# The fill of the window phase: first values into the score banks, second sequence turned behind them, group statistics in later periods

## The reference, cut to what matters

```
x = layernorm(h)                       # no scale: the group statistics of this document
for l in range(2):
    q, k, v = split(shift_token(x) @ wqkv[l])
    q, k = rotary_xpos(l2norm(q) * qs, l2norm(k) * ks)
    x = x + softmax(mask(8 * q @ k.T)) @ v @ wo[l]
    a, g = split((layernorm(shift_token(x)) * lg + lb) @ w1[l] + b1[l])
    x = x + (a * gelu(g)) @ w2[l] + b2[l]
```

## Time and profile before

| what | us |
|---|---|
| median of 3 runs | 1328.47 |
| lowest and highest | 1324.59, 1329.86 |
| profiled execution | 1324.94 |
| its span, first to last instruction | 1323.2 |
| mean granted TensorE clock | 0.981 |

### The profile page before, as it was taken

How to read it: one execution, slowest core, us unless ns; L and a number is a source line. 1 busy time by engine, 2 the same in 40 slices (tenths; PEclk the granted TensorE clock), 3 DMA queues, 4 the chain that set the end, 5 groups by cost and what they waited for, 6 DMA issues and landing times.

```text
span 1323.2 us, 26280 instructions
## 1 busy us (share of the span) xinstructions
PE 1237.8 (94%) x9027; PEld 1055.8 (80%) x9027; DVE 975.9 (74%) x2609; ACT 866.0 (65%) x1987; POOL 629.6 (48%) x694
## 2 busy tenths in 40 slices
PE   5899999999999998899977889999999999999996
PEld 4799889889988987777755667888888887888786
DVE  5767666766667675998887897778778788777633
ACT  2455766675566654889943567677777787777753
POOL 7423431341235233555234567556656567666442
PEclk9899999999999999999987999999999999999999
DMA  7300010010000001110020002000100000000000
GB/s 167 110 1 14 1 63 0 14 63 0 0 8 1 1 1 57 17 55 10 17 68 1 1 5 84 11 5 5 48 4 3 20 5 13 21 21 21 21 17 25
DMA packets 35489, 33.19 MB, mean 25 GB/s; under 512 B 12474, under 2 KB 32050, under 8 KB 35378
## 3 DMA queue, kind: packets, MB, share of 16 engines
q1 hardware_dynamic: 34482, 29.65, 7.5%
q0 software_dynamic: 768, 2.10, 0.9%
q10 hardware_dynamic: 128, 0.04, 0.0%
HBM read 25.75 MB, written 4.19 MB: 23 GB/s over the span
## 4 chain that ended last, share of the span: by engine, by line
PE 44%; DVE 7%; issue 4%; POOL 3%; ACT 3%; DVEq 0%; ACTq 0%; POOLq 0%
PE w_ps_p L1866 3%; PE w_ring L1926 3%; PE w_ring L1927 3%; PE w_ring L1928 3%; PE w_ring L1836 2%; PE w_ring L1838 2%; PE w_ring L1837 2%; PE w_ps_a L1884 2%; PE w_ps_d L1859 2%; PE w_ps_d L1856 2%; PE w_ring L1938 2%; PE a_ps L903 2%; PE w_ring L1843 2%; PE w_ring L1939 1%; PE w_ring L1940 1%
## 5 line engine op out<-in xcount | busy, mean ns | idle before, releaser
L377 ACT ACTIVATE t_gf<-t_ps_f,t_fb_cur 128x512 f32<-128x512 f32 x128 | 87.9, 687 | 169.9 <-PE t_ps_f L283 166.7
L296 PE MATMUL t_ps_o<-t_w_hi,t_g_hi 128*128 128x256 f32 x512 | 146.7, 287 | 3.3 <-DVE t_g_lo L527 3.2
L527 DVE TENSOR_TENSOR t_g_lo<-t_gf,t_g_hi 128x512 fp32r<-128x512 f32 x128 | 93.8, 735 | 70.6 <-ACT t_g_hi L379 69.4
L298 PE MATMUL t_ps_o<-t_w_hi,t_g_lo 128*128 128x256 f32 x512 | 145.3, 284 | 0.0
L297 PE MATMUL t_ps_o<-t_w_lo,t_g_hi 128*128 128x256 f32 x512 | 145.3, 284 | 0.0
L680 POOL TENSOR_TENSOR t_rs<-t_ve,t_neghalf 128x4 f32<-128x4 f32 x32 | 35.0, 1094 | 170.8 <-DVE t_ve L488 169.3
L2431 DVE COPY w_pt<-w_ps_p 128x384 f32<-128x384 f32 x128 | 70.5, 551 | 62.0 <-PE w_ps_p L1866 60.6
L1926 PE MATMUL w_ring<-w_nh,w_w_hi 128*128 128x256 f32 x352 | 104.2, 296 | 6.9 <-DVE w_nl L2475 5.2
L2652 POOL TENSOR_TENSOR w_m<-w_m 128x512 f32<-128x512 f32 x64 | 85.5, 1336 | 40.2 <-DVE w_m L2388 40.1
L296 PEld LDWEIGHTS t_ps_o<-t_w_hi,t_g_hi 128*128 128x128 f32 x512 | 98.3, 192 | 7.8 <-issue 4.5
L281 PE MATMUL t_ps_f<-t_nh,t_w_hi 128*128 128x512 f32 x256 | 102.7, 401 | 1.4 <-DVE t_nl L503 1.0
(11 more groups left out here) (310 smaller groups left out, 4324.8 us busy)
## 6 DMA issues: line engine op xcount, KB each, us to landing
t_raw<-in_L_tok_w SPq DMA_DIRECT2D x8, 1024.0 KB
out<-X SPq DMA_DIRECT2D x14, 256.0 KB, 2.1
raw<-in_L_ffn_wqkv SPq DMA_DIRECT2D x2, 1536.0 KB, 6.6
raw<-in_L_ffn_w SPq DMA_DIRECT2D x4, 640.0 KB, 4.9
w_raw_o<-out SPq DMA_DIRECT2D x8, 256.0 KB, 2.8
w_xs<-X SPq DMA_DIRECT2D x14, 127.0 KB
w_raw<-in_L_ffn_w SPq DMA_DIRECT2D x2, 640.0 KB
t_raw_d<-in_L_tok_D SPq DMA_DIRECT2D x4, 256.0 KB
```

Of the source, the lines that this page charges most:

```text
L296: pe.matmul(out, g_hi[:, j % 4, tok], w2_hi[:, j, :], start=(j == 0 and t % 2 == 0), stop=False, skip_group_check=True)
L298: mm = pe.matmul(out, g_lo[:, j % 4, tok], w2_hi[:, j, :], start=False, stop=(j == FC - 1 and t % 2 == 1), skip_group_check=True)
L527: dve.tensor_tensor(g_lo[:, j % 4, :], gf[:, j % 2, :], g_hi[:, j % 4, :].bitcast(F32), ALU.subtract).then_inc(g_split, 1)
```

## The change

1. In period 1 the values of item 0 go into the two score banks (`first_values`), right behind the last key projection, and no longer wait for the rotation. ACT takes them from there (`keep_first`).
2. The turning of item 1 follows at once; ACT `spread(1, 0)` stands ahead of `root(0, 1)`, DVE `split_in(1, 0)` ahead of `inverse_root(0, 1)`, and PE's first query projection of item 1 moves from the start of period 2 to the end of period 1, ahead of the turning of the first keys of item 0.
3. In period 2 the two value projections of item 1 stand behind `scores(1)` and `scores(2)` instead of behind `scores(3)`.
4. Group statistics: `x0_variance(2)` from period 1 to period 2 (behind the inverse roots), `x0_norm(2)` to period 3; `x0_variance(3)` from period 3 to 5, `x0_norm(3)` to period 6; `x0_root(2)` and `x0_root(3)` on POOL accordingly.
5. `fills` is split: the array of maxima is cleared in period 1, the padding in period 2 (`fill` then counts to 2).
6. `hi_2(0)` moves from period 5 to the end of period 4, `lo_2(0)` from period 5 to period 4, between `scale_p(12)` and `scale_p(13)`.
7. Some waits are added where a bank now has another reader before it.

```diff
@@ tensor
+            def first_values(t):
+                tok = slice(t * P, (t + 1) * P)
+                cols = slice(2 * INNER, 3 * INNER)
+                pe.wait_ge(done["y_added"], NSQ)
+                for c in range(DC):
+                    pe.matmul(ps_d[:, t, :], ah[:, c, tok], qkv_hi[:, c, cols], start=(c == 0), stop=False)
+                    pe.matmul(ps_d[:, t, :], ah[:, c, tok], qkv_lo[:, c, cols], start=False, stop=False)
+                    mm = pe.matmul(ps_d[:, t, :], al[:, c, tok], qkv_hi[:, c, cols], start=False, stop=(c == DC - 1))
+                mm.then_inc(S["v_full"], 1)
...
-                if real(b):
-                    pe.wait_ge(S["split1"], b + 1)
+                if real(b) and h != 2:
                     pe.wait_ge(S["split1"], b + 1)
                     project(b, 0, 0, 0, "q_full")
...
+                    pe.wait_ge(S["k_read"], 2 * c + 2)
...
+                        pe.wait_ge(S["q_read"], 2 * c + 2)
...
+                    pe.wait_ge(S["v_done"], 2 * c + 2)
...
                     scores(NU * c + 1)
+                if h == 2:
+                    pe.wait_ge(S["k_read"], 2 * b + 2)
+                    project(b, 0, 2, 3, "v_full")
...
                     scores(NU * c + 2)
+                if h == 2:
+                    pe.wait_ge(S["q_read"], 2 * b + 2)
+                    project(b, 1, 2, 2, "v_full")
...
-                if real(b):
+                if h == 1:
+                    first_values(0)
+                    first_values(1)
+                elif real(b) and h != 2:
                     ...
                     project(b, 0, 2, 3, "v_full")
...
-                if real(b):
+                if real(b) and h > 2:
                     ...
                     project(b, 1, 2, 2, "v_full")
+                if h == 1:
+                    pe.wait_ge(S["split1"], 2)
+                    project(a, 0, 0, 0, "q_full")
@@ scalar
+            def keep_first(t):
+                act.wait_ge(S["v_full"], t + 1)
+                act.activation(v[:, t, :], ps_d[:, t, :], ACT.Copy).then_inc(S["v_done"], 1)
...
+                if h == 1:
+                    keep_first(0)
+                    keep_first(1)
+                    spread(1, 0)
                 if real(b):
                     root(b, 1)
...
-                if h == 5:
-                    hi_2(0)
...
                     turned(b, 0, 1, 1)
+                if h == 4:
+                    hi_2(0)
@@ vector
                     add_attention(e, 0)
+                if h == 6:
+                    x0_norm(3)
...
                     clamp(b, 1)
+                if h == 1:
+                    fill_maxima()
+                if h == 3:
+                    x0_norm(2)
+                if h == 5:
+                    x0_variance(3)
...
+                if h == 1:
+                    split_in(a, 0)
                 if real(b):
                     inverse_root(b, 1)
                 if real(d):
                     output_lo(NU * d + 3)
+                if h == 2:
+                    x0_variance(2)
                 if real(c):
                     turned_p(H * c + 2)
-                if real(a):
+                if h == 2:
+                    fills()
+                if real(a) and h != 1:
                     split_in(a, 0)
...
-                if h == 1:
-                    x0_variance(2)
-                if h == 1:
-                    x0_norm(2)
-                if h == 3:
-                    x0_variance(3)
-                if h == 3:
-                    x0_norm(3)
@@ gpsimd
-                if h == 1:
-                    x0_root(2)
                 if real(b):
                     scale_k(b, 1)
+                if h == 5:
+                    x0_root(3)
                 if 0 <= f < M - 1:
                     hidden_lo(f, 0)
-                if h == 5:
-                    lo_2(0)
...
                 if real(b):
+                    if h == 2:
+                        x0_root(2)
                     scale_p(NU * b + 0)
+                    if h == 4:
+                        lo_2(0)
                     scale_p(NU * b + 1)
```

More of the change, by code:

```diff
@@ L2124, in hi_2 @@
                 act.wait_ge(S["h_used"], NSQ * FC * l)
-                act.wait_ge(S["fill"], 1)
+                act.wait_ge(S["fill"], 2)
                 act.activation(w2_hi[0:LAST, FC - 1, :], raw_2[0:LAST, FC - 1, :], ACT.Copy)
@@ L2316, in half @@
                     output_hi(NU * d + 3)
-                if real(b):
+                if real(b) and h != 1:
                     keep_values(b, 0, 3)
@@ L2612, in fills @@
             def fills():
-                dve.wait_ge(done["y_full"], NSQ)
                 for w in (w1_hi, w1_lo):
@@ L2618, in fills, with fill_maxima @@
                 for w in (w2_hi, w2_lo):
-                    dve.memset(w[:, FC - 1, :].bitcast(F32), 0.0)
+                    ins = dve.memset(w[:, FC - 1, :].bitcast(F32), 0.0)
+                ins.then_inc(S["fill"], 1)
+            def fill_maxima():
+                dve.wait_ge(done["y_full"], NSQ)
                 dve.memset(mx[:, :, :], 0.0).then_inc(S["fill"], 1)
                 dve.wait_ge(S["fill"], 1)
-            return half, pads, table, fills, x0_variance, x0_norm, split_in, rotate
+            return half, pads, table, x0_variance, x0_norm, split_in, rotate
         def gpsimd(pool):
@@ L2716, in half @@
                     hidden_lo(f, 1)
-                if h == 3:
-                    x0_root(3)
                 if h == 8:
@@ L2865, in _ @@
                 early_half, _, first = a_vector(dve)
-                half, pads, table, fills, x0_variance, x0_norm, split_in, rotate = w_vector(dve)
+                half, pads, table, x0_variance, x0_norm, split_in, rotate = w_vector(dve)
                 first()
@@ L2880, in _ @@
                 rotate(0, 0, 1, 1)
-                half(1)
-                fills()
-                for h in range(2, M3 + 6):
+                for h in range(1, M3 + 6):
                     half(h)
```

## The result

The changed kernel takes 1313.02 us (median of 4 runs, 1308.42 to 1315.75) against 1328.66 for the kernel before (4 runs, 1324.59 to 1329.86): a ratio of 0.989, interval 0.986 to 0.992. It is faster, by 1.1%, and the forecast of 1312 is 1 us off, closer than runs that spread over 7 us can tell. Timed again later it gave 1312.97 (6 runs) against 1325.82, ratio 0.990 (0.988 to 0.993). The profiled execution took 1310.7 with a span of 1308.9, 14.3 less than the profiled execution before, where the sum of the prediction was 14.8.

A forecast was written before the change was run, and what follows sets the result against it. PE was taken as the bound from period 6 on, with the fill's gain moving everything behind it. Terms 7.6 + 4.9 - 1.2 + 3.5 = 14.8 us gave 1310.1 or 1313.7; forecast 1312 us, range 1307 to 1321.

The forecast's parts named there:

- The values and the first projection of item 1: Period 1: PE can project item 1 at 697.1 where it started at 702.14, 5.0 us earlier.
- Rotation of item 1: Period 2: DVE starts to rotate item 1 at 700.5 instead of 707.1, 6.6 us earlier.
- `split_in` of item 2 at about 722: End of period 2: item 2 split at about 722 instead of 730.07; fill gain taken as 7.6 us.
- the low-clock rival: Clock stays low in the new fill, which then brings only 3.0 us; 1314.7 to 1318.3 us, chance 0.17.
- Group 3: Period 3 into 4: its statistics and normalization no longer precede the softmax; gain 4.9 us (3.2 to 4.9).
- `hi_2`: Period 4: ACT's copies ahead of item 4's first squares delay DVE's rotations; loss 1.2 us (0 to 1.9).
- `lo_2`: Period 5: it no longer holds back `scale_p(14)`, removing PE's 2.04 us wait and low clock; gain 3.5 us (2.0 to 3.7).
- `x0_variance(3)` and `x0_norm(3)`: Periods 5 and 6: the moved pieces cost 0, up to 1.2 us and up to 2.1 us respectively.
- `x0_norm(2)`: Period 3: needs 1.38 us and fits where DVE is idle for 2.11 us, ahead of 750.76.
- the skeptical case: Period 3: by the port-lock rule the moved normalization could take 2.1 us or start late; 2.1 still fits into 2.11.
- the one with the wait for `split1`: Period 1: this wait on item 1 replaces the removed one; 7.2 us less gain, 1318 to 1321 us, chance 0.05.
- the one with DVE as the bound: DVE bounds the whole start and moved pieces come back; 8.4 us less gain, or 3.8 left, 1321 to 1324; chance 0.12.

The follow-up runs named there:

- values alone: Kernel before with only item 0's values moved into the score banks, without the earlier turning and with group 2 where it was: 1325.1 us, ratio 0.997.
- the second trace: Changed kernel run once more, unchanged, on the chip of a later comparison: 1312.97 us, ratio 0.990 to the kernel before.
- both halves: Changed kernel with hi_2(0) and lo_2(0) put back in period 5: 1319.53 us, ratio 0.994 to the kernel before.
- best version: Changed kernel with group 2's statistics, root and fills in period 3, normalization in period 4: 1309.03 us, ratio 0.985; again 1310.37 us, ratio 0.987.
- the kernel with the low half back: Changed kernel with only lo_2(0) back in period 5, hi_2(0) staying in period 4: 1315.54 us, ratio 0.991 to the kernel before.

## Why the prediction was right, step by step

- *The values and the first projection of item 1* were to start at 697.1; they did at 696.91, with 1.74 us of wait where 1.9 was worked out. Putting the values back into the ring brings PE's 3.65 us back. Right.
- *Rotation of item 1* at 700.5, measured 700.16; *first softmax* at 706.9, measured 706.19. Right, within 0.7 us. That it needs group 2 gone was shown twice: with the values alone the second interval gives back 2.6 of 4.0 us, and group 2 back in period 1 costs a 3.24 us wait and the clock.
- *`split_in` of item 2 at about 722*, measured 721.69 + 0.40 = 722.09, a gain of 8.0. The working had come to 8.1 and took 7.6 of it without saying why. In part this was luck: `soft` began 0.7 earlier than worked out, and from there to the end of the split it took 15.9 us instead of 15.0. What I did not count is what happens right behind: the hole of 716 to 722 leaves a clock of 0.66 for 5 us and the next wait (1.71 us at 738.01) one of 0.76 for 7 us. Item 3 is split only 6.8 us earlier (748.7 against 755.5), and only 5.6 in the second trace (750.0). The term was too large by 0.8, or by 2.0, and no step of mine had this; the low-clock rival had the mechanism, but in the stretch before.
- *Group 3*, 4.9 taken: the wait at 797.59 stands at 786.54, 11.05 us earlier, which is 4.2 more than at item 3's split (4.6 in the second trace); putting it back cost 4.4 to 4.8. Mechanism right, size 0.1 to 0.7 too large.
- *`hi_2`*, a loss of 1.2 taken: nothing was lost. The wait of PE is 0.95 us at 786.54 against 0.96. The rows for this stand below the list.
- *`lo_2`*, 3.5 taken: the span is 14.3 us shorter and the scores at 799.04 came 11.0 earlier, so 3.3; by the fifth and sixth intervals it is 3.6, and 3.6 in the kernel with that edit alone. Right in this pair of traces; "values alone" shows that about 1.5 of it is a low clock that need not come. It ran at 794.86 to 798.46 in POOL's idle time (795.55, 2.91 us), and PE waited 0.26 us behind it, as at this place before. The step did not say that this gain and the free place of `x0_root(3)` depend on each other; undoing `lo_2` costs 4.8, and both halves 5.7, not 3.5.
- *`x0_variance(3)` and `x0_norm(3)`* at no cost: the fifth and later intervals are those of the kernel that has group 3 elsewhere (31.6 and 35.9 in both). *`x0_norm(2)`* took 2.17 us at 741.79, beside POOL's two scalings from 741.24, as the skeptical case had it (2.1), and no wait of PE of more than 0.22 us follows up to 752.54: right, though no run moved it alone.

  The rule of the Trainium skill, SBUF — State Buffer, section "Who interferes with whom", that DVE and GpSimd lock each other out of a shared port pair, agrees with this row and with the 1.22 us that 16 elements took at 697.45 beside POOL's 1.30 from 697.34.
- *The sum.* 6.8 + 4.2 + 0 + 3.3 = 14.3, against 7.6 + 4.9 - 1.2 + 3.5 = 14.8. Three terms were 0.2 to 0.8 too large, and one loss of 1.2 did not come, so the sum is nearer than its parts. That it is only 0.5 off is luck; the steps are right by their mechanism and to about 1 us each. Of the rivals, the one with the wait for `split1` is out (1.74 us, not 3.67), the one with DVE as the bound is out for the later periods, but true of one place, the hole in period 2, worth 3.5 to 4.6 us.
- *Readings of the rows.* Two were slightly off, without weight in the sum: one of PE's waits in period 2 (0.73 us at 710.45 before) was not for DVE, and the two small steps behind the statistics took 0.38 and 0.47 us at 756.87 before, not 0.55 together.

The delay by `hi_2` was there at first. Item 4's first rotation starts at 778.72, 9.99 us earlier than in the kernel before (788.71), while ScalarE's rounding just ahead of it (773.53 against 784.65) came 11.1 earlier: it is 1.1 late. It was won back a few rows on. The kernel before, VectorE and then GpSimd, in period 4:

```profile
793.89 1.00 DVE L2471 SCALAR_TENSOR_TENSOR w_nmr<-w_mv,w_rs 128x2 f32<-128x2 f32 x1
794.82 0.66 DVE L2396 TENSOR_SCALAR w_sc<-w_ss 128x16 f32<-128x16 f32 x1
795.58 0.69 DVE L2376 TENSOR_REDUCE w_ss<-w_m 128x8 f32<-128x512 f32 x1
```

```profile
792.36 2.51 POOL L2652 TENSOR_TENSOR w_m<-w_m 128x512 f32<-128x512 f32 x2
```

The changed kernel, VectorE, the same three pieces of work:

```profile
783.76 0.59 DVE L2504 SCALAR_TENSOR_TENSOR w_nmr<-w_mv,w_rs 128x2 f32<-128x2 f32 x1
784.27 0.16 DVE L2429 TENSOR_SCALAR w_sc<-w_ss 128x16 f32<-128x16 f32 x1
784.54 0.69 DVE L2409 TENSOR_REDUCE w_ss<-w_m 128x8 f32<-128x512 f32 x1
```

Two tiny operations on DVE took 1.00 and 0.66 us before, and 0.59 and 0.16 after. Before, the first ended at 794.89, as POOL's 2.51 us from 792.36 did, at 794.87. By 784.54 (795.58 before) the stream is 11.04 earlier again. That the later rotations only met POOL at another moment is my reading; no run tests it. The cost of 0 was in the range taken for `hi_2`, but for a reason that I did not have.

What stays open: the clock. It fell behind the hole at 716 to 722, and behind a wait of 2.04 us in the kernel before, but not behind the same wait of 2.03 us in "values alone"; this is read from the rows, not explained. Whether what is missing from group 3 is clock or DVE was not tried.

## What to carry to other kernels

In the fill of a pipeline the order of one queue decides: look for the first wait of the bounding engine, then at what stands in the releaser's queue that no one needs yet, and move both together, since the first without the second gained 4.0 us in one interval and returned 2.6 in the next. Put a movable piece into a period where the idle bracket ahead of the next needed operation is longer than the piece, and count all pieces that end up ahead of the same reader: the root (1.02 us) alone cost nothing there, `lo_2` (0.73 and 2.96) alone made PE wait 2.0 us, and both together 3.2. When medians of a few runs cannot tell versions apart, compare the times between marks inside the phase, and learn first from two traces of one kernel which of these intervals scatter.

## What the runs showed besides

- Runs of one kernel scatter over 4 to 11 us. The best version's twelve lie six at 1305.7 to 1307.8 and six at 1312.0 to 1313.7. Part of it lies ahead of the window phase, in code that no edit touches: the first rounding starts at 677.9 and 679.0 us in the two traces of the changed kernel, and at 684.2 and 685.3 in the two of the best version, both of which are from its slower six. One stretch where the clock differs is 550 to 600 us. The first row is the second trace of the changed kernel, the second the best version; at 0.90 a fifth of 50 us ran at half speed, which by estimate loses 5 us of the 6.3 between these two.

```profile
550.00:600.00 50.00, 47.32 (x450) 36.90 (x442) 48.48 (x117) 45.20 (x98) 27.09 (x36) 1.00 0.13 36
```

```profile
550.00:600.00 50.00, 46.50 (x411) 35.16 (x412) 45.17 (x104) 41.74 (x87) 26.50 (x35) 0.90 0.12 36
```

- A PE wait of 3 us cost a third to a half more than its length in these traces, with the low clock behind it: in period 4 the wait was 3.16 us and its removal was worth 4.2 to 4.6; in the kernel with the low half back it was 3.24 and cost 4.8. A wait of 2.0 us made its interval 2.8 us longer where the clock fell and 1.3 where it did not.
